# Attention of a ViT tower: a third score bank, outputs and maxima turned without TensorE, and another order of a step

## The reference, cut to what matters

```
attn = einsum('bnhd,bmhd->bhnm', q * scale, k)      # 32 heads in all (b, h), each 1024 x 1024
attn = softmax(attn + bias[None], axis=-1)
out  = einsum('bhnm,bmhd->bnhd', attn, v).reshape(Bw, Nw, Cd)
return out @ proj_w + proj_b                        # then h = h + this, layernorm, experts
```

## Time and profile before

| | before |
|---|---|
| median of 3 runs | 698.26 us (697.87 to 698.61) |
| the profiled execution's own time | 700.25 us |
| its span | 698.5 us |
| PE busy (share of span) | 653.6 us (94%) |
| DVE busy | 485.8 us (70%) |
| ACT busy | 379.2 us (54%) |
| POOL busy | 74.4 us (11%) |
| TensorE clock granted, mean | 0.951 |

### The profile page before, as it was taken

One profiled execution on the slowest core, in us unless ns is written; L12 is line 12 of the kernel. 1 busy time (PEld: TensorE's weight loads), 2 busy tenths in 40 slices (PEclk: granted clock), 3 DMA queues, 4 the chain that ended last, 5 costly groups with the idle time before them and its releaser, 6 DMA issues. The chain is left out here.

```text
span 698.5 us, 13275 instructions
## 1 busy us (share of the span) xinstructions
PE 653.6 (94%) x4374; PEld 216.6 (31%) x4374; DVE 485.8 (70%) x631; ACT 379.2 (54%) x712; POOL 74.4 (11%) x186
## 2 busy tenths in 40 slices
PE   9999899876699999999999999999999976999997
PEld 4323233222122333333333333333323322333332
DVE  4354453636978888888888888888886658574543
ACT  2102212021377777777777778787877624465443
POOL 8501010101200000000000000000000202000000
PEclk9999998975599999999999999999999977999999
DMA  8200554041411212121212121212120020200000
GB/s 301 58 3 0 151 143 130 22 115 49 139 37 37 74 37 73 36 72 36 72 36 72 36 72 36 72 36 72 36 73 3 1 61 0 56 20 8 17 8 15
DMA packets 42961, 40.46 MB, mean 58 GB/s; under 512 B 21777, under 2 KB 32178, under 8 KB 42930
## 3 DMA queue, kind: packets, MB, share of 16 engines
q1 hardware_dynamic: 42930, 40.05, 20.1%
HBM read 26.16 MB, written 11.58 MB: 54 GB/s over the span
## 5 line engine op out<-in xcount | busy, mean ns | idle before, releaser
L805 DVE TENSOR_REDUCE nmax<-ps 128x1 f32<-128x1024 f32 x256 | 311.7, 1222 | 54.7 <-PE ps L1139 38.4
L639 ACT ACTIVATE probs<-ps 128x512 f32<-128x512 f32 x512 | 278.0, 595 | 100.6 <-PE ps L1233 73.4
L1248 PE MATMUL ps<-probs,v_ring 128*32 128x256 f32 x2048 | 166.0, 397 | 0.0
L1233 PE MATMUL ps<-q_ring,k_ring 51*128 51x512 bf16 x512 | 156.5, 392 | 2.8
L1139 PE MATMUL ps<-k_ring,q_ring 48*128 48x512 bf16 x512 | 133.7, 399 | 9.7 <-DVE nmax L805 9.6
L1233 PEld LDWEIGHTS ps<-q_ring,k_ring 51*128 51x128 bf16 x512 | 43.5, 93 | 127.6 <-ACT probs L639 91.2
L1040 DVE TENSOR_TENSOR probs<-probs,ps 128x512 f32<-128x512 f32 x64 | 41.2, 683 | 46.6 <-ACT probs L708 46.5
L1122 PE MATMUL ps<-g_t,x_all 96*128 96x512 f32 x128 | 65.0, 626 | 5.2 <-DVE gated L820 5.2
L1248 PEld LDWEIGHTS ps<-probs,v_ring 128*32 128x32 f32 x2048 | 40.7, 108 | 92.8 <-issue 78.9
L708 ACT ACTIVATE probs<-ps,wide_w 128x512 f32<-128x512 f32 x64 | 40.4, 683 | 47.4 <-PE ps L1400 47.3
L820 DVE TENSOR_TENSOR gated<-ps,gamma_sb 128x512 f32<-128x512 f32 x64 | 42.6, 686 | 32.3 <-PE ps L1122 32.2
(11 more groups left out here) (174 smaller groups left out, 438.9 us busy)
## 6 DMA issues: line engine op xcount, KB each, us to landing
k_ring<-qk_parts SPq DMA_DIRECT2D x64, 96.0 KB, 2.4
q_ring<-qk_parts SPq DMA_DIRECT2D x64, 96.0 KB, 2.4
gamma_sb<-gamma_t SPq DMA_DIRECT2D x4, 1024.0 KB, 10.0
v_padded<-v_pad SPq DMA_DIRECT2D x4, 1024.0 KB, 4.7
v_ring<-v_padded SPq DMA_DIRECT2D x32, 128.0 KB, 2.8
qk_parts<-qk_h SPq DMA_DIRECT2D x8, 384.0 KB, 4.3
x_ring<-bias_parts SPq DMA_DIRECT2D x32, 96.0 KB, 3.1
qk_parts<-qk_m SPq DMA_DIRECT2D x8, 256.0 KB, 3.9
```

The costliest lines, as they stand in the source:

```text
L639: A.activation(probs[:, s % 4, HALF * j:HALF * (j + 1)], ps[:, S2A + j, :], ACT.Exp).then_inc(exp_done[j], 1)
L805: V.tensor_reduce(nmax[:, par, s:s + 1], ps[:, bank:bank + 2, :].rearrange("p a n -> p (a n)"), AX, ALU.max, negate=True).then_inc(s1_redu ...
L1233: last = mm(ps[:, S2A + j, :], k_ring[rows, u, P * s:P * (s + 1)], q_ring[rows, u, HALF * j:HALF * (j + 1)], start=True, stop=not corner)
L1248: last = mm(ps[VC * j:VC * (j + 1), PVB, 0:2 * P], v_ring[:, u, m, :], probs[:, m % 4, 2 * P * j:2 * P * (j + 1)], start=(m == 0), stop=(m ...
```

## The change

It does these things:

- **Maxima.** `turn_maxima` goes from TensorE to VectorE: a transpose within blocks of 32 x 32 (`max_p` padded to 32 columns), placed after `row_max` of step 1. The copy on ScalarE goes. `max_t` now holds four blocks of rows, so `send_max_rows` issues 8 DMAs instead of 2, of 3 x 4 x 32 elements instead of 3 x 4 x 128.
- **Outputs.** `turn_output` and `normalize` go. SP stores `o_t` of each head to DRAM (`store_output`), and later loads it back with features on partitions (`load_sums`, `load_inverse`), VectorE inverts the sums of a sample, SP stores them and loads them broadcast, POOL multiplies (`scale_attention`).
- **Projection.** One set of 8 small matmuls gives the projection token by token; the bias is added to `h_all` earlier by POOL. `turn_attention`, `turn_projection` and three copies for each sample go. For the last sample it moves behind the first expert matmul.
- **Third bank.** The lower half by key now alternates between two banks (`key_bank`), the upper half has a third, so that the lower half of step `s + 1` is computed with the upper half of step `s`. `PVB` moves to bank 7.
- **Order of a step** on TensorE: by key, values, by query (before: by key, by query, values). The wait for `max_rows` of head `g + 1` now stands before step 7 of head `g`.

The core of the diff:

```diff
-        max_p = sb("max_p", [P, 2, 2, PARTS, NT // 2], bf16)
-        max_t = sb("max_t", [PARTS * NT, P], bf16)
-        o_t = sb("o_t", [P, 2 * P], fp32)
+        SQ = VC
+        max_p = sb("max_p", [P, 2, SQ], bf16)
+        max_t = sb("max_t", [P, 2, SQ], bf16)
+        o_t = sb("o_t", [P, 2, 2 * P], fp32)
...
-        S1A, S2A, PVB, MISC = 0, 4, 6, 7
+        N_MAX_ROWS = 16 * 8
+        S1A, S2A, PVB = 0, 4, 7
+        def key_bank(s, j):
+            return S2A + (2 if j else s % 2)
...
-            def send_max_rows(n, u):
-                sp.wait_ge(max_copied, n + 1)
-                half = PARTS * NT // 2
+            def send_max_rows(turned, par, u):
+                sp.wait_ge(max_turned[par], turned + 2)
                 for j in range(2):
-                    sp.dma_start(q_ring[UPPER * j + ROWS:UPPER * j + MAXROWS, u, HALF * j:HALF * (j + 1)],
-                                 max_t[half * j:half * (j + 1), :]).then_inc(max_rows[u], 16)
+                    for a in range(4):
+                        rows = q_ring[UPPER * j + ROWS:UPPER * j + MAXROWS, u, HALF * j:HALF * (j + 1)].rearrange(
+                            "i (m a r) -> i m a r", a=4, r=SQ)
+                        first = SQ * a + PARTS * NT // 2 * j
+                        sp.dma_start(rows[:, :, a, :], max_t[first:first + PARTS * NT // 2, par, :]
+                                     ).then_inc(max_rows[u], 16)
+
+            def store_output(copied, par, g, u):
+                sp.wait_ge(o_copied[u], copied)
+                sp.dma_start(o_scratch[ds(g, 1), :, :].rearrange("o x (j q) -> o j x q", j=4), o_t[:, par, :]
+                             ).then_inc(o_stored[par], 16)
+
+            def load_sums(b):
+                sp.dma_start(sums[:, b, :], o_scratch[NH * b:NH * (b + 1), DH, :].rearrange("h (r q) -> h r q", q=D)
+                             ).then_inc(sums_loaded[b // (B - 1)], 16)
+                for j in range(2):
+                    sp.dma_start(ao_all[D * j:D * (j + 1), b, :],
+                                 o_scratch[NH * b:NH * (b + 1), 0:DH, HALF * j:HALF * (j + 1)]
+                                 ).then_inc(ao_loaded[b // (B - 1)], 16)
...
             def attend_sp(it, first, last):
                 for u in range(RING):
                     if not (last and u == RING - 1):
-                        send_max_rows(it * RING + (u + 1), (u + 1) % RING)
+                        send_max_rows(it * 2 + (u + 1) // 2, (u + 1) % 2, (u + 1) % RING)
+                    if not (first and u == 0):
+                        store_output(it + (2 if u else 1), (u - 1) % 2, it * RING + (u - 1), (u - 1) % RING)
                     if not (first and u == 0) and not (last and u > 0):
-                        sp.wait_ge(o_copied[(u - 1) % RING], it + (2 if u else 1))
                         load_head(it * RING + (u - 1 + RING), (u - 1) % RING)
+                    if last and u == 0:
+                        for i in range(2):
+                            sp.wait_ge(o_stored[i], 16 * (G - NH) // 2 + 1)
+                        for b in range(B - 1):
+                            load_sums(b)
+                    if last and u == 1:
+                        for b in range(B - 1):
+                            store_inverse(b)
+                        for b in range(B - 1):
+                            load_inverse(b)
...
             attend_sp(G // RING - 1, False, True)
+            store_output(G // RING + 1, (RING - 1) % 2, G - 1, RING - 1)
+            for i in range(2):
+                sp.wait_ge(o_stored[i], 16 * G // 2 + 1)
+            load_sums(B - 1)
+            store_inverse(B - 1)
+            load_inverse(B - 1)
...
+            def turn_maxima(n, par, sent):
+                dve.wait_ge(max_split, n + 1)
+                if sent is not None:
+                    dve.wait_ge(max_rows[sent[0]], sent[1])
+                V.transpose(max_t[:, par, :], max_p[:, par, :]).then_inc(max_turned[par], 1)
...
                             row_max(g + 2, s, u % 2)
-                        if s == 5 and not (first and u == 0):
-                            normalize(g - 1)
+                        if s == 1 and not (last and u == RING - 1):
+                            sent = (u - 1) % RING
+                            turn_maxima(g + 1, (u + 1) % 2, None if first and u == 0 else
+                                        (sent, it * N_MAX_ROWS + (N_MAX_ROWS if u else 0)))
...
+            WITHIN = {(2, 2): [(project_attention, 0)], (2, 4): [(project_attention, 1)],
+                      (2, 7): [(project_attention, 2)], (3, 0): [(turn_norm, 0)], (3, 4): [(turn_norm, 1)]}
...
                     start, end = first and u == 0, last and u == RING - 1
-                    pe.wait_ge(max_rows[u], it * 32 + 32)
+                    v = (u + 1) % RING
                     pe.wait_ge(values_loaded[u], it * 16 + 16)
                     if ahead:
                         pe.wait_ge(operands[(u + 2) % RING],
                                    (it + (u + 2) // RING) * (16 * N_OPERANDS) + 16 * N_OPERANDS)
+                    if start:
+                        pe.wait_ge(max_rows[u], N_MAX_ROWS)
+                        scores_by_key(0, u, 0)
                     for s in range(NT):
+                        if s == NT - 1 and not end:
+                            pe.wait_ge(max_rows[v], (it + (u + 1) // RING) * N_MAX_ROWS + N_MAX_ROWS)
                         for j in range(2):
-                            scores_by_key(g, s, u, j)
-                        if ahead:
-                            scores_upper(g + 2, s, (u + 2) % RING)
-                            scores_lower(g + 2, s, (u + 2) % RING)
+                            pe.wait_ge(exp_done[j], g * NT + (s + 1))
+                        scores_by_key(s, u, 1)
+                        if s + 1 < NT:
+                            scores_by_key(s + 1, u, 0)
+                        elif not end:
+                            scores_by_key(0, v, 0)
                         if s == 0 and not start:
                             values(it, g - 1, NT - 2, (u - 1) % RING)
                         if s == 1 and not start:
                             values(it, g - 1, NT - 1, (u - 1) % RING)
                         if s > 1:
                             values(it, g, s - 2, u)
-                        if s == 1 and not end:
-                            if not (first and u < 2):
-                                pe.wait_ge(o_normed, g - 1)
-                            turn_maxima(g + 1, (u + 1) % 2)
-                        if s == 4 and end:
-                            pe.wait_ge(o_normed, g - 1)
-                        if s == 4 and not start:
-                            turn_output((u - 1) % RING, it + (2 if u else 1), G if end else g + 2)
+                        if ahead:
+                            scores_upper(g + 2, s, (u + 2) % RING)
+                            scores_lower(g + 2, s, (u + 2) % RING)
```

218 lines of the change are left out of this document (105 added, 113 removed).

## The result

The changed kernel takes 920.18 us (median of 4 runs, 916.14 to 922.98) against 698.07 us before (4 runs, 692.31 to 698.61): the ratio is 1.320, 95% interval 1.312 to 1.329. It is slower, as forecast, but by 222 us where I had said 182, and the time lies 5 us above the range.

The account below looks back on a forecast made before the run. Bound before: engines taking close turns in an 11.6 us head, SP's queue loop nearly as long at 11.27. Periods +174, start +2, last heads -7, tail +13 make +182 on 700.25: 882, 880 for the median; range 770 to 915.

Parts of the forecast that it names:

- the ring through SP's queue: Loop from turned maxima through sends, store and loads to the next head's start: 11.27 us before, 17.8 us forecast.
- the store of the outputs: SP's store between the sends and the loads in each head: taken as 0.45 us with its gap.
- the landing of `x_ring`: Time from issue of the last load that the next head waits for to its landing: 3.1 us.
- the last heads: Heads 29 to 31, to the last output's copy: 39.5 us instead of 46.6, so -7 (-15 to +5).
- Third bank and order: Attention steps: up to 1.5 us a head to save, counted at nothing because SP's loop covers it.
- Issue of a send: SP's time to issue one send of maxima: 0.75 us (0.3 to 0.9), eight a head, 6.0 us.
- the cheap rival: Smaller sends issue in 0.45 us, as a load does: 765 us at full clock, 812 at low; chance 0.14.
- the rival at 675 us: Sends cost SP next to nothing, so VectorE or the short chain sets a 10.5 us period; chance 0.06.
- From the head's start to turned maxima: TensorE's first scores and values, VectorE's maxima and transpose: 4.3 us at full clock, 6.0 at low.
- Periods: Heads 2 to 29, 28 periods of 17.8 us instead of 11.6: +174 us.
- Tail: From the last output's copy to the logits, input parts behind the last sample's round trips: +13 us (8 to 18).
- Full clock: Rival: TensorE's clock does not fall, or rises before VectorE's second maximum: 832 us; chance 0.22.

Follow-up runs that it names:

- e1: Kernel before with only its two sends of the maxima split into eight: 861.19 us (before 697.29).
- e2: Changed kernel with the four lower-half sends cut in two, twelve sends a head instead of eight: 1000.29 us.
- e6: Changed kernel with the store of the previous head's output moved behind the ring's loads on SP's queue: 883.89 us.
- e11: e10 with the third bank gone, two banks and the old order of by-key scores: 694.55 us, ratio 0.998 to the kernel before.
- e10: e8 together with e7's edit, and by-query scores ahead of the values again: 667.15 us, ratio 0.962 to the kernel before.
- e12: Changed kernel with the four upper-half sends issued from ScalarE's queue instead of SP's: 823.87 us.
- e5: Changed kernel with eight unread matmuls at the top of each head and eight ahead of step 7: 878.19 us.
- e7: Changed kernel with the input parts of samples 0 and 1 placed ahead of the last head's output store: 903.26 us.
- e8: Changed kernel with eight sends replaced by one store to memory and two loads, maxima turned after step 0's maximum, output store last: 683.9 us.
- e3: Changed kernel with VectorE's turn of the maxima ahead of a head's first row maximum instead of behind the second: 790.82 us.

## Why the prediction was right and wrong

**The step that failed.** The mechanism was right, the ring through SP's queue; three terms of the sum were mis-sized: the store of the outputs (14 us), the landing of `x_ring` (11) and the last heads (11). They are 36 of the 40 us that I missed.

**The bound before.** Right: SP's ring left 0.3 us, and what was put into it was paid almost at once (e1, e2, e6). What I had only named in passing, that the engines take turns closely over the banks, was what set the 11.6 us (e11).

**Third bank and order, counted at nothing.** Right for the changed kernel: e1 without them and e6 with them have the same period within 0.1 us, both bound by the ring. The saving of up to 1.5 us a head that I set behind the ring exists: e10 has 1.2 of it.

**Issue of a send, 0.75 us.** Right: eight took 6.00 us in their row, and e2's smaller pieces were no cheaper (0.70 us each), which excludes the 0.45 of the cheap rival. The Trainium skill ("DMA: Bandwidth & Descriptors", Issuing engines are not separate DMA queues) calls a dispatch usually small relative to the DMA itself; here eight of them are a third of the head, and the rival at 675 us that I drew from it fell by 245 us. The same section says that starting DMAs from several engines saves only this starting time; e12 agrees, and here that "only" is 96 us.

**The store of the outputs, 0.45 us.** Mis-sized, the first failed term. It takes 0.64 us, and from the last send to the first load it is 1.16, where my sum had 0.45 + 0.21. I had taken my value from the store of `v_padded`. +0.5 us a head, 14 us.

**The landing of `x_ring`, 3.1 us.** Mis-sized a little: 3.5 us from its issue to TensorE's restart. The median of the page ends at the landing and not at the first instruction behind it, and some 0.3 us of it came only with the store ahead of the loads (e6). +0.4 us, 11 us. The chain as a whole, from the turn's end at 408.18 to 420.84, took 12.7 us where I had summed 11.8.

**From the head's start to turned maxima.** Right: to the turn's end 6.1 us measured, 6.0 forecast for the low clock; e5 has 4.2 at the full one, forecast 4.3. That the head starts at 1.2 GHz after two lulls was right in the heads shown here.

**Periods.** 18.71 for 17.8: the two terms above. +25 of the 40 us that I missed.

**Start, last heads, tail.** Start -1.4 for +2. Last heads +4.3 for -7; the corners of heads 30 and 31 stand 23.2 and 14.8 us behind the ones before them. By the starts of by-key scores head 29 took 14.8 us (720.58 to 735.38) as forecast, but head 30 20.3 for 14 and head 31, to the output's copy at 771.75, 16.1 for 11. Head 30's projection waits for the scaled outputs, as forecast, but starts 10.1 us into the head, not 7.5:

```profile
745.45 1.97 PE L1323 MATMUL ps<-wide_w,ao_all 64*128 64x64 f32 x16 [6.08 <-POOL ao_all L606]
```

(My sum had slipped too: 12.0 + 3.3 + 5.1 is 20.4, not 21.) How the remaining steps of both heads divide their excess, no run here separates. Tail +16.6 for +13, inside its range, and e7 shows that my mechanism was the right one: the parts stand behind the round trips. The rest, +2.8, was not in the sum.

**The range.** Its upper end added 34 us for a slower issue to the forecast; it did not add to this the ends of store, landing, last heads and tail, which all erred to one side. Its lower end is 5 us above my own price for the cheap send at full clock, 765.

**The rivals.** Full clock (832) fell: the clock was 0.69 in the heads. Even a kernel that works through its waits (e5, clock 0.92) takes 878. Cheap send fell. "The loads are no wait" fell: 26 waits, 97 us.

## What to carry to other kernels

Count the dispatches on each DMA queue inside the loop that closes from one iteration to the next, at some 0.7 us for a small transfer of many short pieces (here the same from 16 to 128 columns): e1 shows that six more of them made a kernel 24% slower without touching one computation. When a layout change (here a turn in blocks of 32) splits a transfer, look for an address pattern that joins the pieces again, even by way of memory, before spreading them over queues. And before giving an edit up, undo its costly part alone: with three dispatches in place of eight, the turn, the store and the parts in other places, this change takes 0.965 of the time before.

## What I had not expected

- A send's issue is 698 ns at the median for pieces of 16 and of 32 columns and 720 for 128 columns; the loads from memory of the same rows (e8's) take 732. The store of 128 x 32 takes 344 ns, the store of 4 x 32 x 256 takes 637.
- Two bounds within 0.3 us of each other in the kernel before (11.59 for the two banks, 11.27 for SP's ring): a trial that shortens the ring alone (e11) gives next to nothing, and the two together give 29 us (e10).
- In the ring over two heads that an earlier turn made (e3), short and long heads alternate; the mean of 14.1 us, which no head has, hides it.
- Doing 16 useless matmuls in each head made the kernel 42 us faster (e5), since they kept TensorE at 2.4 GHz in most heads.
